# The state of 24 units turned by VectorE and DRAM instead of TensorE; row sums and bias additions moved to GpSimd

## The reference, cut to what matters

```python
x = norm(x + (adj @ (x @ W0) + b0))                     # layer 0
x = norm(x + ((si + sj + adj*w_r + g_b) @ x) @ W1 + b1) # layer 1
x_h = elu(x @ Wi + bi)                                  # layer 2, attention
e = sigmoid(a_tgt[:, :, None] + a_src[:, None, :] + be) * mask
recv = concat([e @ x_h, x_h * sum(e, -1)]); recv = elu(recv @ Wn + bn)
x = norm(x + concat([recv, x_h]) @ Wm + bm)
for _ in range(5):                                      # layer 3, a gated recurrence
    m = adj @ h
    z = sigmoid(m @ W3 + h @ U3 + ...); r = sigmoid(m @ W4 + h @ U3 + ...)
    h = (1 - z) * h + z * tanh(m @ W5 + (r * h) @ U5 + ...)
x = norm(x + h)
```

## Time and profile before

| | us |
|---|---|
| median of 3 runs | 1265.48 (1264.34 to 1265.53) |
| the profiled execution | 1264.36 |
| its span, first to last instruction | 1262.6 |

### The profile page before, as it was taken

The page is one execution under the profiler, slowest core; times in us unless marked ns, Lnnn a source line. Parts: engine busy times, 40 slices in busy tenths (PEclk is TensorE's granted clock), DMA queues, the critical chain, the costliest instruction groups (busy, mean ns, idle before and its releaser), DMA issues.

```text
span 1262.6 us, 15547 instructions
## 1 busy us (share of the span) xinstructions
PE 1217.9 (96%) x5488; PEld 935.6 (74%) x5488; DVE 870.5 (69%) x2037; ACT 683.0 (54%) x1109; POOL 73.2 (6%) x79
## 2 busy tenths in 40 slices
...
DMA packets 38476, 52.71 MB, mean 42 GB/s; under 512 B 2752, under 2 KB 19648, under 8 KB 38400
## 3 DMA queue, kind: packets, MB, share of 16 engines
...
q0 software_dynamic: 144, 0.40, 0.1%
...
## 4 chain that ended last, share of the span: by engine, by line
PE 85%; DVE 7%; ACT 3%; issue 2%; POOL 1%; SPq 1%; DMA 1%; POOLq 0%; DVEq 0%; ACTq 0%
PE ps L613 45%; PE ps L618 7%; PE ps L620 7%; PE ps L619 7%; PE ps L710 6%; PE ps L631 4%; PE ps L624 4%; ACT x L883 2%; DVE ring L1227 1%; PE ps L702 1%; PE ps L716 1%; PE ps L723 1%; PE ps L724 1%; PE ps L672 1%; PE ps L691 1%
## 5 line engine op out<-in xcount | busy, mean ns | idle before, releaser
L613 PE MATMUL ps<-adj_hi,xh 128*128 128x512 f32 x672 | 293.1, 436 | 2.0 <-DVE ml L1078 1.6
L613 PE MATMUL ps<-adj_hi,xl 128*128 128x512 f32 x672 | 263.4, 392 | 0.0
L613 PE MATMUL ps<-adj_lo,xh 128*128 128x512 f32 x672 | 262.7, 391 | 0.0
L613 PEld LDWEIGHTS ps<-adj_hi,xh 128*128 128x128 f32 x672 | 126.7, 189 | 41.8 <-issue 18.6
L613 PEld LDWEIGHTS ps<-adj_lo,xh 128*128 128x128 f32 x672 | 126.9, 189 | 35.9 <-issue 13.9
L613 PEld LDWEIGHTS ps<-adj_hi,xl 128*128 128x128 f32 x672 | 126.4, 188 | 27.8
L878 ACT ACTIVATE mh<-ps 128x512 fp32r<-128x512 f32 x80 | 47.7, 597 | 135.7 <-PE ps L613 135.5
L710 PE MATMUL ps<-ring,fz 128*128 128x512 f32 x224 | 112.6, 607 | 4.5 <-DVE ring L1227 4.4
L1252 DVE TENSOR_TENSOR r<-r,hT 128x512 f32<-128x512 f32 x80 | 54.4, 691 | 88.9 <-ACT r L990 88.9
L1227 DVE TENSOR_TENSOR ring<-ring,mk 128x512 f32<-128x512 f32 x128 | 87.2, 686 | 35.1 <-ACT ring L933 35.1
L618 PE MATMUL ps<-mh,wh 128*128 128x512 f32 x240 | 102.1, 425 | 1.4 <-DVE ml L1078 1.3
...
## 6 DMA issues: line engine op xcount, KB each, us to landing
mk<-mask_scratch SPq DMA_DIRECT2D x128, 256.0 KB, 2.7
...
```

The lines of the kernel that those rows point to most:

```text
L613: mm = pe.matmul(dst, a[:, t, :], b[:, t, cut(h)], start=(t == 0 and i == 0), stop=(t == T - 1 and i == 2))
```

## The change

The units whose `prev` is one of the first four steps of one of the first three pairs (`by_dma`: units 1 to 8, 11 to 18 and 21 to 28, 24 in all, two halves each) no longer turn the state on PE. DVE transposes the new half of `hT` in 32x32 blocks into `v` (one STREAM_TRANSPOSE of 128x512), SP sends `v` to a scratch tensor in DRAM (256 KB) and fetches it back in four DMAs of 64 KB, one per group of 32 partitions, into `tl` of the stream; ACT and DVE make `xh` and `xl` from there, at the same places of their orders as before. The product of the next unit waits for `xl` half by half, and `candidate_start` for the tanh instead of `xl`. The other 16 turns (i = 4 or p = 3) stay on PE.

The row sums and both bias additions go from DVE to POOL. All tables are written anew: SP has one too (`k..` is the load of a mask tile), and the attention of each batch is spread over more units.

```diff
     "PE": """ ...
+unit4 @15 t2b:3 pja:3 @17 pjb:3 @22 tha:3 thb:3 @23 tga:3
+unit12 @10 sums:4 @16 rows:4 @21 y1a:4 @24 y1b:4
+unit17 @2 y2b:4 @9 t2a:5 t2b:5 @19 pja:5 pjb:5 @22 tha:5 @25 thb:5 @26 tga:5 tgb:5
+unit22 @10 rows:6 @21 y1a:6 @22 y1b:6
+unit27 @7 t2a:7 t2b:7 @19 pja:7 pjb:7 @22 tha:7 @25 thb:7 @26 tga:7 tgb:7
...
+        def by_dma(p, i):
+            return not is_last(i) and p + 1 < PAIRS
+        def blocks(s, h):
+            return tl[s][:, cut(h)].bitcast(F32).rearrange("p (c t j) -> p c t j", c=4, j=32)
...
+            def send_state(s, h, p, i):
+                sp.wait_ge(blocks_turned, nth_but(p, i, s, h))
+                sp.dma_start(state_dram[s, h], v[:, cut(h)]).then_inc(s_sent[s][h], 16)
+            def fetch_state(s, h, p, i):
+                sp.wait_ge(s_sent[s][h], 16 * (p * (STEPS - 1) + i + 1))
+                for a in range(4):
+                    sp.dma_start(tl[s][32 * a:32 * a + 32, cut(h)].bitcast(F32).rearrange("p (c n) -> p c n", c=4),
+                                 state_dram[s, h].rearrange("(c i) (a n) -> i c a n", c=4, a=4)[:, :, a, :]
+                                 ).then_inc(s_turned[s][h], 16)
+            def unit(now, prev, before, fill):
+                fill()
+                if before and is_last(before[2]):
+                    ...            # store of a finished batch, load of the next
+                fill()
+                turning = prev and by_dma(*prev[1:])
+                for go in (send_state, fetch_state):
+                    for h in range(2):
+                        if turning:
+                            go(prev[0], h, *prev[1:])
+                        fill()
...
+            def add_bias(b, row, name):        # POOL; in the place of c0 and c2
+                x = x_of(b)
+                tell(pool.tensor_tensor(x[:, :, :], x[:, :, :], row.unsqueeze(1).to_broadcast([P, T, D]), ALU.add),
+                     name, b)
...
+                elif name[0] == "s" and name[1:].isdigit():   # POOL
+                    ...
+                    seen(pool, "ma" + name[1:], b)
+                    tell(pool.tensor_tensor(f["r"][:, cut(h)], before, ring[:, k % RING, :], ALU.add),
+                         "rs_" + name[1:], b)
...
-                    pe.wait_ge(xl_done, nth(p, i - 1, s, 1))
+                    pe.wait_ge(xl_done, nth(p, i - 1, s, 0))      # half 1 is waited for at tile 4
...
                 def turning():
-                    if prev:
+                    if prev and not by_dma(*prev[1:]):
                         turn_state(prev[0], 0, *prev[1:])
...
             def state_hi(s, h, p, i):
-                if not is_last(i):
-                    act.wait_ge(t_done, nth(p, i, s, h))
+                if by_dma(p, i):
+                    act.wait_ge(s_turned[s][h], 16 * 4 * (p * (STEPS - 1) + i + 1))
+                    copy(by_block(xh[s], h), blocks(s, h)).then_inc(xh_done, 1)
...
                     dve.tensor_tensor(hT[s][:, cut(h)], v[:, cut(h)], hT[s][:, cut(h)], ALU.subtract).then_inc(h_new, 1)
+                    if by_dma(p, i):
+                        dve.wait_ge(h_new, nth(p, i, s, h))
+                        dve.transpose(v[:, cut(h)].rearrange("p (a t j) -> p a t j", a=4, j=32),
+                                      hT[s][:, cut(h)].rearrange("p (t a i) -> p a t i", a=4, i=32)
+                                      ).then_inc(blocks_turned, 1)
...
-                        tell(dve.tensor_tensor(f["r"][:, cut(h)], first_sum, ring[:, k % RING, :], ALU.add),
-                             "rs_" + name[1:], b)
```

More of the change, by code:

```diff
@@ L30 @@
 TABLES = {
[L31 to L42, removed]
@@ L46 @@
+unit6 @3 k13:3 @4 k14:3 @5 k15:3 k16:3 k17:3
+unit7 @5 k00:4 k01:4 k02:4
 unit8
 unit9
[L48 to L66, removed]
+unit10
+unit11
+unit12
+unit13 @5 k03:4 k04:4
```

344 lines of the change are left out of this document (219 added, 125 removed).

## The result

Before 1264.96 us (1264.04 to 1266.31), after **1268.83 us** (1265.66 to 1272.16), nine runs each: ratio 1.0026, 95% interval 1.0014 to 1.0039. The change costs 0.3%, where I forecast a gain of 1.4%.

What follows compares the result with a forecast made beforehand. PE, 96% busy, was taken to bound the kernel by its instruction count. 1264.4 - 21.4 + 3.0 + 0.5 + 1 - 2 = 1245.5 profiled, 1247 us as median; own range 1238 to 1257, 8-in-10 range 1237 to 1266.

Steps and rivals of the forecast that it cites:

- What goes, 21.4: Between 205 and 1080 us, 48 turns leave PE at 0.445 us each, saving 21.4 us.
- the turns were hidden: Rival: PE's transposes only filled pipeline slack, gain 17 instead of 21.4, 1251 us; no chance of its own given.
- The rest of PE's work stays: the tables hold the same pieces.: PE's other work is unchanged and the other 32 turns stay on PE; no cost was entered.
- N = 3.2: Cover, in us of other PE work, needed before the second update gate to hide the DRAM round trip; bounds 2.3 to 7.
- Missing cover 3.0 + 0.5: PE's waits where pieces fall short: 3.0 us over units 17, 22, 27, 12; 0.5 in unit 6 behind a mask load.
- The first 205 us, -2: Row sums and bias on POOL, up to 205 us: a gain of 2 us, between 8 gained and 12 lost.
- GpSimd's additions, +1: POOL's additions beside DVE in the round trip's chain cost 1 us, range 0 to 8.
- the lock rival: DVE and POOL lock each other, attention tiles come every 2.1 instead of 1.40 us: 1258 us, chance 0.12.
- the trip outlasts its cover: Rival: PE waits at the second update gate for the round trip; decides from N = 5.4, 1273 us at 6; chance 0.14.
- The tells: Profile signs expected if the forecast held: counts of transposes, busy times, waits, gaps and operation lengths.
- PE between 250 and 1060 us idle for over 10 us: Sign, in the stretch where PE had almost no gaps, that the forecast sum is wrong.
- unit 0 over 8 us later: Sign that the sum is wrong: unit 0 starts over 8 us later than before.

Runs made afterwards that it cites:

- 9: Kernel before with only the changed kernel's order of pieces within units 0 to 39, all turns on PE: 1279.4 us, ratio 1.0112.
- 14: Changed kernel with old order ahead of unit 0, sums and bias on DVE, blocks read directly without DRAM (state not the reference's): 1254.0 us, ratio 0.9915.
- 4: Changed kernel with the old order ahead of unit 0 and row sums and bias additions back on DVE: 1263.7 us, ratio 0.9988.
- 3: Changed kernel with the old order of pieces ahead of unit 0, all else as changed: 1261.7 us, ratio 0.9973.
- 5: Kernel before with 24 units turned by DVE and DRAM, mask loads placed around the trip, other tables old: 1341.7 us, ratio 1.0606.
- 13: Changed kernel without the way through DRAM, blocks read directly from v (state not the reference's): 1258.6 us, ratio 0.9946.
- 7: Kernel before with only the changed kernel's order of pieces ahead of unit 0: 1274.7 us, ratio 1.0081.
- 11: Kernel before with 96 idle additions more on GpSimd, 12 in each of units 31 to 38: 1306.3 us, ratio 1.0324.
- 16: Kernel before with only the row sums moved to GpSimd, bias additions staying on DVE: 1275.1 us, ratio 1.0087.

## Why the prediction was wrong

The path from before to after, one edit at a time, from the table: new order in the units +14.8 (9); turns off PE -24.9 (14); the way through DRAM +9.0 (4); sums and bias to GpSimd -2.0 (3, barely told); new order ahead of unit 0 +7.0 (changed kernel). The sum is +3.9, and so it must be; the single steps hold in this sequence. In the old order the turns by DMA alone cost 77.2 (5).

- *What goes, 21.4.* Right, if anything low: 24.4 and 24.9. The excess would be waits that the turn on PE makes in the new order, such as the 3.2 for `xl` in 9; that is argued, not shown. The rival "the turns were hidden", 17, is refuted for this order.
- *"The rest of PE's work stays: the tables hold the same pieces."* **This step failed, and weighs most.** The pieces are the same, but they were moved to stand between candidate and second gate. I used their new places as cover and took their price as nothing; it is 14.8 with the turns on PE (9). With the turns gone and the trip free, 14 gains 10.1 of the 21.4, so 11.3 of the price remain.
- *N = 3.2.* Right where nothing else stands (2.8 to 3.1), and the transpose of 0.69 (0.71) with it. In the fetch two errors cancel, which is luck: a landing of 2.7 was 2.0 to 2.1, and SP's hold of 0.32 for each of the four was 0.43 in the median.
- *Missing cover 3.0 + 0.5.* **Mis-sized:** 9.0 to 9.5. Two causes are in the rows: in units with masks and sums N grows, to 5.4 in unit 5, by a mask load, a slower fetch and a stretched `xl`; and the second fetch, which I gave no wait, makes 2.2 us of waits for `z`, which 13 does not have. PE waits for `ml` in units 1, 4, 5, 6, 12, 17, 27 and 28; in 17 and 27, where I missed 1.0 each, it is 0.5, and in 22, where I missed 0.9, nothing to speak of.
- *The first 205 us, -2.* **Failed by 11.** I priced GpSimd's pace there; what costs is the new order: 7.0 taken back by 3, 10.2 added by 7. It came half as gaps and half as longer busy time under a lower clock (5.1 and 3.9 above; 5.4 and 5.2 in 7). By windows of 10 us from 20 to 200 us the changed kernel loses at most 10.3 us to the clock, the one before 3.4. I had no term for the clock anywhere.
- *GpSimd's additions, +1 and the lock rival.* In the changed order they gain 2.0 to 4.6. The lock is real, 0.43 us for each addition in 11, the lower clock included. The 112 sums cost 11.0 in the old order (16), where the lock and the slower addition are not told apart; in the new one both are outweighed by what DVE is rid of.
- *Rival "the trip outlasts its cover"* named the right mechanism. I gave it 0.14, as I asked whether one N exceeds 5.4 everywhere.
- *The tells.* Transposes 128: yes. PE busy 1196: 1207.6. Waits for `ml` 3 to 4 us: 5.8, of which 1.0 stands in unit 39 as before. GpSimd near 230 us: 275.3. Gaps from 30 to 205 us near 13: 20.2. DVE's mask products at 1.5 and more would show the lock: their mean is 818 ns, so some were held. "PE between 250 and 1060 us idle for over 10 us" (10.9) and "unit 0 over 8 us later" (9.0): both came, and both pointed at the failed steps.
